# Rows that carry their pair's number through the expert stage of a four-layer graph network

## What is computed

```python
new_feats = _gcn_conv(feats, edge_src, edge_dst, W_conv, b_conv)
scores = x @ gate_W + gate_b                       # x is new_feats
topv, topi = jax.lax.top_k(scores, 2)
gw = jax.nn.softmax(topv, axis=-1)
pos = ...                                          # how many earlier pairs chose this expert
C = 2 * ceil(P / E); valid = pos < C               # P = 25000 pairs, E = 64: C = 782
slot = eid * C + where(valid, pos, 0)
buf  = zeros((E * C, d)).at[slot].add(x_rep)       # rows sorted by expert
hact = gelu(buf @ W1[e] + b1[e])                   # 128 -> 256
y    = hact @ W2[e] + b2[e]                        # 256 -> 128
y_pairs = y[slot] * valid
core = gw[0] * y_pairs[:, 0] + gw[1] * y_pairs[:, 1]
out  = batchnorm(new_feats + core)
```

## Time and profile before

| | |
|---|---|
| median of three runs | 7797.86 us |
| profiled execution | 7827.45 us, its span 7825.8 us |
| busy: PE, DVE, ACT, POOL | 5224.2, 3840.1, 1999.1, 5056.1 us |
| DMA moved | 1010.29 MB |
| sending, expert stage, fetching and combining | 334, 316, 288 us |

### The profile page before, as it was taken

The page is one execution under the profiler, slowest core; times in us unless marked ns, Lnnn a source line. Parts: engine busy times, 40 slices in busy tenths (PEclk is TensorE's granted clock), DMA queues, the critical chain, the costliest instruction groups (busy, mean ns, idle before and its releaser), DMA issues. The chain is left out here.

```text
span 7825.8 us, 128830 instructions
## 1 busy us (share of the span) xinstructions
PE 5224.2 (67%) x33115; PEld 3591.5 (46%) x33116; DVE 3840.1 (49%) x17648; ACT 1999.1 (26%) x5522; POOL 5056.1 (65%) x4249
## 2 busy tenths in 40 slices
PE   2666666666666676078888426900788884888886
PEld 1555555555555554055544325700454442554444
DVE  6776666776777776622332453325223325223325
ACT  2333333444444554311111002302111112011003
POOL 1888888888888888266666452165666663666662
PEclk6888888888888888589999658955899996899998
DMA  9666666666667766666655105713455553455552
GB/s 224 60 75 72 71 78 80 85 90 92 95 97 99 104 108 101 208 207 211 211 183 170 49 32 142 191 46 97 157 169 174 172 173 112 156 166 176 171 173 85
DMA packets 947027, 1010.29 MB, mean 129 GB/s; under 512 B 212803, under 2 KB 830889, under 8 KB 946592
## 3 DMA queue, kind: packets, MB, share of 16 engines
q0 software_dynamic: 308320, 270.50, 25.9%
q1 hardware_dynamic: 284610, 545.10, 21.7%
q10 hardware_dynamic: 353662, 189.69, 8.3%
HBM read 641.73 MB, written 345.71 MB: 126 GB/s over the span
## 5 line engine op out<-in xcount | busy, mean ns | idle before, releaser
L795 POOL DMA_INDIRECT sums<-work,idx x1564 | 2485.2, 1589 | 612.6 <-issue 300.9
L763 POOL DMA_INDIRECT work<-table,src_t x2097 | 1994.7, 951 | 1139.3 <-issue 560.2
L1309 PE MATMUL pp<-shared 128*128 128x504 bf16 (+6 forms) x10584 | 2225.5, 363 | 620.2 <-issue 246.3
L1309 PEld LDWEIGHTS pp<-shared 128*128 128x128 bf16 x10584 | 1044.5, 104 | 1622.4 <-issue 681.7
L1743 DVE TENSOR_TENSOR acc<-acc,pp 128x80 f32 x525 | 124.8, 238 | 1717.8 <-remote 1108.3
L1207 PE MATMUL pp<-acc 128*128 128x130 f32 x3128 | 538.9, 325 | 364.3 <-ACT work L958 294.2
L1292 PE MATMUL pp<-work 128*128 128x80 f32 x4194 | 612.6, 284 | 220.5 <-issue 130.0
L1292 PEld LDWEIGHTS pp<-work 128*128 128x128 f32 x4194 | 600.6, 204 | 318.8 <-issue 266.8
L1207 PEld LDWEIGHTS pp<-acc 128*128 128x128 f32 x3128 | 470.6, 229 | 382.5 <-issue 382.5
L975 ACT ACTIVATE shared<-pp 128x490 bf16<-128x490 f32 (+11 forms) x1128 | 570.6, 547 | 130.8 <-PE pp L1246 97.4
L1029 ACT ACTIVATE shared<-shared 128x128 bf16<-128x128 f32 x588 | 179.2, 305 | 1559.9 <-issue 652.6
(11 more groups left out here) (328 smaller groups left out, 6925.0 us busy)
## 6 DMA issues: line engine op xcount, KB each, us to landing
shared<-counts SPq DMA_DIRECT2D x126, 882.0 KB
shared<-counts SPq DMA_DIRECT2D x126, 840.0 KB
work<-table,src_t POOLq DMA_INDIRECT x2097
shared<-counts SPq DMA_DIRECT2D x42, 798.0 KB
shared<-counts SPq DMA_DIRECT2D x42, 787.5 KB
shared<-counts SPq DMA_DIRECT2D x42, 735.0 KB
shared<-counts SPq DMA_DIRECT2D x42, 714.0 KB
expert_rows<-zeros ACTq DMA_DIRECT2D x66, 392.0 KB
```

What stands on the lines that cost most here:

```text
L763: pool.indirect_dma_start(out=msg[:, i % SLOTS, k, :], out_offset=None, in_=table, in_offset=bass.IndirectOffsetOnAxis(ap=src_t[:, at:at + ...
L795: pool.indirect_dma_start(out=sums0[table], out_offset=bass.IndirectOffsetOnAxis(ap=picked, axis=0), in_=rows, in_offset=None, compute_op= ...
L1309: i = pe.matmul(bank[c][:, 0:COLS[n]].rearrange("p (k w) -> p k w", w=PACK * w), x3[:, b % 2, h, part3, :], ring[:, q % RING, 0:TB * COLS[ ...
```

## The change

Each row of `expert_rows` becomes 129 elements wide (`XW`), 516 bytes: the last element is the number of the pair (choice k of node number n is k x 12544 + n). The buffer is cleared with zeros and, in the last element, the number 1048576 (`FAR`), which lies out of bounds of any pair. A new DRAM buffer `pair_rows` (25088 rows of 128) takes the answers in order of pairs; ACT clears it with 14 more plain DMAs during the neighbour sums. In sending, DVE writes the new features into rows of 129 elements, and ACT copies them for the second choice and adds the pair numbers (two more activations a block), and only then may POOL send. In the expert stage DVE copies the four pair numbers of each partition out of the loaded rows, and POOL scatters the answers to `pair_rows` by four indirect DMAs of 98 rows a unit; rows with the number `FAR` are dropped by the bounds check. ACT's store of a unit is gone, and ACT now loads the second bias. After the experts, SP loads the answers of a block by two plain DMAs (`load_pairs`); POOL's fetch, and DVE's copy of indices for it, are gone. The units keep 392 rows.

```diff
+XW = D + 1
...
-        expert_rows = nc.dram_tensor("expert_rows", [EROWS, D], f32).ap()
+        expert_rows = nc.dram_tensor("expert_rows", [EROWS, XW], f32).ap()
+        pair_rows = nc.dram_tensor("pair_rows", [2 * NPAD, D], f32).ap()
...
-        e_rows, e_y = e_part((QUAD, UT, D)), e_part((QUAD, UT, D))
+        e_rows, e_y = e_part((QUAD, UT, XW)), e_part((QUAD, UT, D))
+        e_pair = e_part((QUAD, UT)).bitcast(i32)
...
+        send_x = part(work, 2 * BW, (2, 2, TB, XW))
...
-                after(sp, e_up, u - (QUAD - 1))
+                after(sp, e_down, u - (QUAD - 1))
...
+            def load_pairs(b, s, turn):
+                after(sp, k_sum, b - 1)
+                for k in range(2):
+                    sp.dma_start(slot[:, 2 * s + k, :, :],
+                                 pair_rows[k * NPAD:(k + 1) * NPAD, :].rearrange("(p t) d -> p t d", p=P)[:, tiles(b), :]).then_inc(k_in[s], 16)
+            further = sp.value_load(quads, min_val=0, max_val=NE * UPE // QUAD - 2)
+            for s in range(QUAD):
+                apart(sp, e_out[s], 16 * UT * further + 32 * UT)
+            batches(sp, load_pairs)
...
+            pool.memset(zeros[:, D:XW], float(FAR)).then_inc(pool_const, 1)
...
+            pool.iota(pair_id, [[NPAD, 2], [1, NT]], base=0, channel_multiplier=NT,
+                      allow_small_or_imprecise_dtypes=True).then_inc(pool_const, 1)
...
+                apart(pool, c_kept, b + 1)
                 for j in range(TB):
                     for k in range(2):
                         pool.indirect_dma_start(
                             out=expert_rows, out_offset=bass.IndirectOffsetOnAxis(ap=send_row[:, s, 2 * j + k:2 * j + k + 1], axis=0),
-                            in_=slot[:, 2 + s, j, :], in_offset=None,
+                            in_=send_x[:, s, k, j, :], in_offset=None,
                             bounds_check=NE * CROWS - 1, oob_is_err=False).then_inc(sent[s], 16)
             batches(pool, send)
 
 
-            def unit_bias(u, s, q):
-                e = pool.value_load(unit_row[0:1, ds(u, 1)], min_val=0, max_val=NE - 1)
-                if not isinstance(u, int):
-                    apart(pool, e_yup, u - (QUAD - 1))
-                pool.dma_start(e_b2[0:EP, s, :], b2e[ds(e, 1), :].rearrange("e d -> (e d)").partition_broadcast(EP))\
-                    .then_inc(b2_in[s], 16)
-            for s in range(2):
-                pool.wait_ge(sent[s], 16 * 2 * TB * (NB // 2))
-            quads_of(pool, unit_bias)
-
-
-            def fetch(b, s, turn):
-                apart(pool, k_idx, b + 1)
-                for j in range(TB):
-                    for k in range(2):
-                        pool.indirect_dma_start(
-                            out=slot[:, 2 * s + k, j, :], out_offset=None, in_=expert_rows,
-                            in_offset=bass.IndirectOffsetOnAxis(ap=fetch_row[:, s, 2 * j + k:2 * j + k + 1], axis=0)).then_inc(k_in[s], 16)
-            further = pool.value_load(quads, min_val=0, max_val=NE * UPE // QUAD - 2)
-            for s in range(QUAD):
-                apart(pool, e_out[s], 16 * further + 32)
-            batches(pool, fetch)
+            def unit_pairs(u, s, q):
+                if isinstance(u, int):
+                    pool.wait_ge(e_yup, u + 1)
+                else:
+                    apart(pool, e_yup, u + 1)
+                for t in range(UT):
+                    pool.indirect_dma_start(
+                        out=pair_rows, out_offset=bass.IndirectOffsetOnAxis(ap=e_pair[0:EP, s, t:t + 1], axis=0),
+                        in_=e_y[0:EP, s, t, :], in_offset=None,
+                        bounds_check=2 * NPAD - 1, oob_is_err=False).then_inc(e_out[s], 16)
+            quads_of(pool, unit_pairs)
...
-                    act.dma_start(rows, zeros[0:EP, 0:D].unsqueeze(1).to_broadcast([EP, FILL, D])).then_inc(buffers_zero, 16)
+                    act.dma_start(rows, zeros[0:EP, 0:XW].unsqueeze(1).to_broadcast([EP, FILL, XW])).then_inc(buffers_zero, 16)
+                    if turn < NB:
+                        pairs = pair_rows[ds(turn * 2 * BW, 2 * BW), :].rearrange("(p t) d -> p t d", p=P)
+                        act.dma_start(pairs, zeros[:, 0:D].unsqueeze(1).to_broadcast([P, 2 * TB, D])).then_inc(buffers_zero, 16)
...
-                act.activation(acc[:, ds(b * BW, BW)], slot_w[:, 2 + s, :], ACT.Copy).then_inc(c_kept, 1)
+                act.activation(send_x[:, s, 1, :, 0:D], send_x[:, s, 0, :, 0:D], ACT.Copy)
+                act.activation(send_x[:, s, :, :, D], pair_id[:, :, tiles(b)], ACT.Copy)
+                act.activation(acc[:, ds(b * BW, BW)].rearrange("p (t d) -> p t d", d=D), send_x[:, s, 0, :, 0:D], ACT.Copy).then_inc(c_kept, 1)
                 act.wait_ge(c_scores, b + 1)
                 act.activation(c_small[:, s, 1, 0:TB], c_small[:, s, 0, 0:TB], ACT.Exp).then_inc(c_exp, 1)
+            act.wait_ge(pool_const, 4)
             batches(act, keep_new)
 
             def hidden(u, s, q):
                 e = act.value_load(unit_row[0:1, ds(u, 1)], min_val=0, max_val=NE - 1)
                 half = s % 2
+                after(act, e_yup, u - (QUAD - 1))
+                act.dma_start(e_b2[:, s, :], b2e[ds(e, 1), :].rearrange("e d -> (e d)").partition_broadcast(P)).then_inc(b2_in[s], 16)
                 after(act, e_act, 2 * (u - 1))
                 act.copy(e_bias[:, half, :], b1_t[:, :, ds(e, 1)].rearrange("p h e -> p (h e)")).then_inc(e_bias_in, 1)
                 after(act, e_mm2, u - 1)
...
                     act.activation(e_hid[:, half, h, :], pp[1 + half][:, h * 512:h * 512 + UROWS], ACT.Gelu,
                                    bias=e_bias[:, half, h:h + 1]).then_inc(e_act, 1)
 
-            def unit_store(u, s):
-                row = act.value_load(unit_row[0:1, ds(u + P, 1)], min_val=0, max_val=EROWS - UROWS)
-                act.wait_ge(e_yup, u + 1)
-                act.dma_start(expert_rows[ds(row, UROWS), :].rearrange("(t p) d -> p t d", p=EP),
-                              e_y[0:EP, s, :, :]).then_inc(e_out[s], 16)
-
-            def unit_step(u, s, q):
-                hidden(u, s, q)
-                if not isinstance(u, int) or u >= 2:
-                    unit_store(u - 2, (s + 2) % QUAD)
-
-            def last_step(u, s, q):
-                unit_step(u, s, q)
-                if s == QUAD - 1:
-                    unit_store(u - 1, s - 1)
-                    unit_store(u, s)
-            quads_of(act, unit_step, last_step)
+            quads_of(act, hidden)
...
-                    i = dve.scalar_tensor_tensor(slot[:, 2 + s, j, :], node_ps[s][:, j * P:(j + 1) * P],
+                    i = dve.scalar_tensor_tensor(send_x[:, s, 0, j, 0:D], node_ps[s][:, j * P:(j + 1) * P],
...
-                dve.tensor_tensor(kept, pos, valid, ALU.mult).then_inc(c_late, 1)
+                dve.tensor_scalar(c_small[:, s, 8, :], valid, -float(FAR), float(FAR), ALU.mult, ALU.add).then_inc(c_late, 1)
                 own(4)
-                dve.tensor_tensor(by_node(gate[:, tiles(b), :]), two(prob), two(valid), ALU.mult)
-                dve.scalar_tensor_tensor(by_node(pair_row[:, tiles(b), :]), two(top), float(CROWS), two(kept), ALU.mult, ALU.add)\
-                    .then_inc(c_late, 1)
+                dve.tensor_tensor(by_node(gate[:, tiles(b), :]), two(prob), two(valid), ALU.mult).then_inc(c_late, 1)
...
-            def unit_rows(u, s):
+            def unit_rows(u, s, q):
                 dve.wait_ge(e_up, u + 1)
                 after(dve, e_mm1, 2 * (u - 1))
+                after(dve, e_out[s], 16 * UT * q)
+                dve.tensor_copy(e_pair[0:EP, s, :], e_rows[0:EP, s, :, D])
                 dve.tensor_copy(e_rows_t[:, s % 2, :], pp[0][:, s % 2 * 512:s % 2 * 512 + UROWS]).then_inc(e_down, 1)
 
             def unit_answer(u, s, q):
                 dve.wait_ge(e_mm2, u + 1)
                 dve.wait_ge(b2_in[s], 16 * (q + 1))
-                after(dve, e_out[s], 16 * q)
                 dve.tensor_tensor(e_y[0:EP, s, :, :], pp[3][0:EP, s % 2 * 512:s % 2 * 512 + UT * D].rearrange("p (t d) -> p t d", d=D),
                                   e_b2[0:EP, s, :].unsqueeze(1).to_broadcast([EP, UT, D]), ALU.add).then_inc(e_yup, 1)
 
             def unit_steps(u, s, q, ahead=True):
                 if ahead or s + 2 < QUAD:
-                    unit_rows(u + 2, (s + 2) % QUAD)
+                    unit_rows(u + 2, (s + 2) % QUAD, q + (s + 2) // QUAD)
                 unit_answer(u, s, q)
 
             dve.wait_ge(units_ready, 1)
-            unit_rows(0, 0)
-            unit_rows(1, 1)
+            unit_rows(0, 0, 0)
+            unit_rows(1, 1, 0)
             quads_of(dve, unit_steps, lambda u, s, q: unit_steps(u, s, q, False))
 
 
-            def rows_of(b, s, turn):
-                after(dve, k_in[s], 16 * 2 * TB * turn)
-                dve.wait_ge(c_late, C_LATE * NB)
```

(12 more changed lines are left out.)

9 lines of the change are left out of this document (5 added, 4 removed).

## The result

The changed kernel takes **7861.47 us** (median of 4 runs, 7854.98 to 7869.08) beside 7801.59 us of the kernel before (4 runs, 7789.79 to 7807.46): ratio 1.0078, 95% interval 1.0064 to 1.0091. It is slower; the forecast was 7757 us. The profiled execution took 7869.08 us with a span of 7867.4.

A forecast was written before the change was run, and what follows sets the result against it. PE bounds the expert stage, POOL's index DMAs the fetch, and POOL's sends with DVE's chain the sending. Expert stage and combining -54, clearing +15, sending -2 give -41 from 7797.9: 7757 us, range 7680 to 7860.

The forecast's parts named there:

- expert stage: Experts' loop: POOL's 352 scatters at 1.22 us replace PE as the bound, 429.4 us, ending at 5205.8.
- rival 5: Expert loop: stalls like DVE's remote waits in sending (8.99 and 5.20 us) appear, up to +290 us; chance 0.05.
- Rival 4: Expert stage: DVE waits for scatters to land, binding from 3.3 us landing; time near 7790, no change; chance 0.09.
- Its second half: Expert stage: PE with 1.5 us gaps may lose its clock, 6.9 us a unit at half clock; time near 7790.
- Rival 1: Expert stage: 98-row scatter cheap at 0.56 + 0.30 us, PE stays the bound, -171, 7627 us; chance 0.12 with in-between prices.
- rival 2: Expert stage, POOL's L873: gain gone from 1.34 us a scatter; at 1.55 + 0.30, +222, 7979 us; chance 0.08.
- Combining: After the experts: first loads land in 5.2 us, then DVE bounds 14 blocks at 6.9 us, 96.6 us.
- Sending: Sends of 516-byte rows: 0 extra, upper end 57 us; two DVE operations fewer a block save 2 us.
- the estimated 8 us: Sending: by the 4096-byte packet rule a second packet per engine, near 0.08 us a send, 8 us more, sum -33.
- Clearing: ACT's 14 more clearing DMAs, 12.8 MB: five in its first nine tiles cost +15 us; bounds 0 and 41.
- the forecast had 54: Expert stage and combining: DVE's last statistics end at 5310.1 instead of 5364.2 us, a difference of -54.

The follow-up runs named there:

- plain run: Changed kernel with each unit's four index scatters replaced by four plain POOL DMAs to fixed places: ratio 0.9823 to the kernel before, 0.978 on the slower chips.
- wide kernel: Changed kernel with units of 3 tiles of 128 rows instead of 4 of 98: 7149.75 us, ratio 0.9909 to the kernel before; 7793.65 us, 0.9975, on slower chips.

## Why the prediction was wrong

It is the **expert stage** that failed, and in it one assumption: that the stage takes what its slowest engine takes, "POOL takes over as the bound: 352 x 1.22 = 429.4". On the chip of the forecast it took 560.6. The 131 us are two things.

- The term itself: a scatter busy 0.962 us, not 0.92, and 1.267 from issue to issue (median), not 1.22: 352 x 0.047 = 17 us. The duration hardly goes with the rows (0.960 at 98, 0.970 at 128), so that the nearest row, the send at 0.978, would have been better without the part for the rows.
- The other 114 us are POOL's waits for DVE's answers. They come because PE's semaphores rise up to 9.55 us late while POOL issues index DMAs, and ACT and DVE wait for them. That is rival 5, to which I gave 0.05. Its evidence stood in the trace: two stalls of 8.99 and 5.20 us in a turn of sending, where POOL issues index DMAs. I argued against it with the expert stage of before and with the fetch. Neither could show it: in the one POOL issued one plain DMA a unit (the plain run shows that even four do no harm), in the other the engines that would have to wait had little to do. And the fetch did suffer: 278.6 us from first to last on S, 247.1 on Q, for the same 196 fetches of 0.95 us.

Rival 4 looked true in after (DVE's L2071 waits 151.3 us for the DMA) and was not the bound. Its own arithmetic wanted a landing of 3.3 us behind the scatter; measured are 1.1 us (median) and 2.9 at the longest, and on Q the same wait of 296.5 us costs nothing. Its second half was worked out wrongly: at half clock, 6.9 us a unit for PE would have cost 88 x (6.9 - 4.88) = 178 us, some 7935 us and not near 7790. The granted clock did fall, to 0.87, but PE is busy 4.4 us a unit, less than POOL's 4.88; what the lower clock adds to the chain of a late unit is not separated. Rival 1 (a cheap scatter) and rival 2 (1.85 us, or anything over 1.34) fell with the 0.962 us. Rival 2's break-even was right as arithmetic, and the price a scatter really had on S was 559.6 / 352 = 1.59 us; only its place was another.

The other steps held. **Combining**: 105 us from the last scatter, 104 forecast; 6.8 us from block to block where the kernel before gave 6.9, and DVE waits for the data once. DVE's timeline, and its additions by line over the stage:

```profile
5319.64 1.93 DVE L2096 SCALAR_TENSOR_TENSOR work<-work,w_t,acc 128x128 f32<-128x128 f32 x7 [11.55 <-DMA work<-pair_rows]
5326.46 1.91 DVE L2096 SCALAR_TENSOR_TENSOR work<-work,w_t,acc 128x128 f32<-128x128 f32 x7
```

```profile
L2096 DVE SCALAR_TENSOR_TENSOR work<-work,w_t,acc 128x128 f32<-128x128 f32 x98 | 26.8, 345 | 11.6 <-DMA work<-pair_rows 11.6
```

**Sending**: rows of 516 bytes cost nothing. The line of the sends, and POOL's queue in that stage (packets, MB, share of 16 engines):

```profile
L860 POOL DMA_INDIRECT expert_rows<-work,w_t x196 | 191.9, 979 | 199.9 <-issue 126.0 <-DVE w_t L2015 73.9
```

```profile
q0 software_dynamic: 6240, 11.10, 10.6%
```

That is 979 against 978 ns, and 6240 packets for 196 sends, 31.8 each, the same number that before's sending stage has. The packets of rows are 4128 bytes now, where they were 4096. The rule of the Trainium skill ("DMA: Bandwidth & Descriptors", section "SWDGE vs HWDGE vs iDMA") that a packet holds preferably at most 4096 bytes would have had a second packet for eight rows of 516; the trace does not show it, and the estimated 8 us did not come. **Clearing**: 0 instead of 15 us. The first send of the wide kernel, with 12 MB more to clear, came 31 us later. The lower bound was the right one here, and I cannot say from these traces where between the two sizes clearing begins to cost.

On chips of kind Q the mechanism of the forecast is what happens in the expert stage, and the ratio is 0.9972, -23 us instead of -41; but that the total comes near is luck. In the profiles after's stretch from the last send to the last statistics is 4 us shorter than before's (573.9 against 578.0), and the forecast had 54: 21 us more for the scatters, and 29 less to be gained, since the fetch there is faster to begin with. The other 19 us lie ahead of the first send, in parts where the change saves nothing, and no run says why.

What stays open: by what path POOL's index DMAs delay the semaphores on S, whether the profiler, whose semaphore records go missing in the same traces, has a part in it, and what makes a chip one of this kind. Two scatters a unit and the wait for each unit's landing were never run on S.

## What to carry to other kernels

A stage's time is the maximum of its engines' work only while they do not disturb each other. Before index DMAs are moved from a stage in which the other engines idle into one in which all are needed, look in the trace for stretches where POOL issues them densely beside other work: a wait called remote there, or a start long after the named releaser's end, is the sign. Compare it with when the semaphore rose, since a wait called remote can also be one that would be there anyway. Count such DMAs rather than their rows: 288 of 128 rows beat 352 of 98 on both kinds of chip. And where a verdict is under one per cent, ask for it on a second chip: here its sign changed.

## What the runs showed of the hardware

- The same program took 7801 to 7815 us on some chips and 7203 to 7217 on others, 8% apart, with durations of single instructions alike (the scatter 0.960 to 0.963 us).
- An index DMA whose rows all fall outside the table costs POOL as much as one that writes 98 rows (0.961 against 0.962 us); a plain one of 98 rows costs 0.559.
- On chips of kind S semaphores that PE raises rise up to 9.55 us after its matmuls' end beside dense scatters of POOL (170 of 291 by over 1 us), and ACT's gelu starts up to 8.85 us late; beside four plain DMAs a unit the latest rise is 0.02 us late and gelu starts at most 0.04 us late.
- Beside the adding scatters of the first layer, one every 1.86 us, no recorded rise of PE's is over 0.33 us late (400 to 3100 us, before on S).
